# Attention maxima in float16, one product per half batch, and turns of queries, keys and sums in other slots

## What is computed

```python
k_mem, v_mem = jnp.split(memory, 2, axis=2)
Q = _split_heads(query, NUM_HEADS) * dh ** (-0.5)
Kh = _split_heads(k_mem, NUM_HEADS)
Vh = _split_heads(v_mem, NUM_HEADS)
logits = jnp.einsum('bhqd,bhkd->bhqk', Q, Kh) + b
...
weights = jax.nn.softmax(logits, axis=-1)
out = jnp.einsum('bhqk,bhkd->bhqd', weights, Vh)
```

## Time and profile before

| what | value |
|---|---|
| median of 3 runs | 3341.56 us (3337.22 to 3347.16) |
| the profiled execution | 3335.4 us, its span 3333.7 us |
| mean granted clock of TensorE | 0.895 of full speed |
| busy share of the span | PE 77%, DVE 68%, ACT 37%, POOL 28% |
| maxima in l0a | 64.9 to 289.4 us |
| maxima in l2a | 1711.3 to 1888.1 us |
| maxima in l2s | 2046.6 to 2253.4 us |
| maxima in l3a | 2980.9 to 3158.4 us |

### The profile page before, as it was taken

The page is one execution under the profiler, slowest core; times in us unless marked ns, Lnnn a source line. Parts: engine busy times, 40 slices in busy tenths (PEclk is TensorE's granted clock), DMA queues, the critical chain, the costliest instruction groups (busy, mean ns, idle before and its releaser), DMA issues. The chain is left out here.

```text
span 3333.7 us, 58668 instructions
## 1 busy us (share of the span) xinstructions
PE 2558.5 (77%) x21348; PEld 1660.5 (50%) x21348; DVE 2258.7 (68%) x5909; ACT 1245.9 (37%) x2228; POOL 924.7 (28%) x1324
## 2 busy tenths in 40 slices
PE   2997367999424367997989776996799999869962
PEld 1443355666323135886456543443565555546651
DVE  5997745666467434666677777997666555777768
ACT  1886334333122103111346564772322222226611
POOL 3442460100350520112655325871000000024200
PEclk9998689999757678999989987998799999889986
DMA  4330454222322215665631012100100000011001
GB/s 111 114 130 30 161 203 154 76 76 77 114 80 80 76 39 181 221 226 192 215 101 52 17 48 93 47 22 5 61 9 12 1 1 1 6 38 46 21 8 56
DMA packets 158163, 266.84 MB, mean 80 GB/s; under 512 B 22635, under 2 KB 106137, under 8 KB 151876
## 3 DMA queue, kind: packets, MB, share of 16 engines
q1 hardware_dynamic: 131204, 186.97, 16.9%
q0 software_dynamic: 17904, 76.23, 6.8%
q10 hardware_dynamic: 8784, 0.04, 0.2%
HBM read 175.25 MB, written 88.34 MB: 79 GB/s over the span
## 5 line engine op out<-in xcount | busy, mean ns | idle before, releaser
L1380 ACT ACTIVATE l2e_hf<-l2e_H 128x512 f32<-128x512 f32 x208 | 124.2, 597 | 375.9 <-PE l2e_H L1336 375.9
L1416 DVE CAST l2e_hh<-l2e_hf 128x512 f16<-128x512 f32 x208 | 88.7, 427 | 127.1 <-ACT l2e_hf L1380 112.0
L688 DVE TENSOR_REDUCE l0a_mx<-l0a_S 128x2 f32<-128x512 f32 x256 | 164.3, 682 | 11.9 <-PE l0a_S L530 11.2
L1336 PE MATMUL l2e_H<-l2o_hi,l2e_w 128*128 128x512 f16 x576 | 151.8, 382 | 14.9 <-DVE l2e_w L1392 14.9
L637 ACT ACTIVATE l0a_pf<-l0a_ST 128x512 f32<-128x512 f32 x256 | 145.9, 598 | 40.5 <-PE l0a_ST L544 34.8
L228 POOL TENSOR_TENSOR l3in_n_rstd<-l3in_n_sq,all_mhalf 128x8 f32<-128x8 f32 x4 | 6.9, 1724 | 553.8 <-DVE l3in_n_sq L152 553.8
L1336 PE MATMUL l2e_H<-l2e_hh,l2e_w 128*128 128x512 f16 x640 | 155.1, 379 | 0.0
L684 DVE CUSTOM_DVE_ANT_0 l2s_masked<-l2s_S,l2s_mq 128x128 f32<-128x128 f32 (+1 forms) x512 | 150.7, 349 | 6.1 <-PE l2s_S L530 5.7
L1380 ACT ACTIVATE l0e_hf<-l0e_H 128x512 f32<-128x512 f32 x128 | 76.4, 597 | 206.7 <-PE l0e_H L1336 206.7
L1336 PE MATMUL l1e_H<-l1b_hi,l1e_w 128*128 128x256 f16 (+1 forms) x936 | 145.4, 275 | 7.8 <-DMA l1e_w<-packed,all_second_weight_row 7.8
L1418 DVE TENSOR_TENSOR l2e_hl<-l2e_hf,l2e_hh 128x512 f16<-128x512 f32 x208 | 144.0, 692 | 7.2
(11 more groups left out here) (726 smaller groups left out, 7448.6 us busy)
## 6 DMA issues: line engine op xcount, KB each, us to landing
l0e_wf<-in_L_ffn_w SPq DMA_DIRECT2D x16, 1024.0 KB, 7.2
rows<-l0a_zeros SPq DMA_DIRECT2D x16, 640.0 KB, 6.1
l1u_rb<-rows SPq DMA_DIRECT2D x20, 512.0 KB, 4.7
results<-l1e_y SPq DMA_DIRECT2D x39, 256.0 KB, 3.9
l0a_kv<-in_ctx SPq DMA_DIRECT2D x16, 512.0 KB, 4.3
rows<-l0a_zeros SPq DMA_DIRECT2D x16, 512.0 KB
l0d_p_cx<-in_ctx SPq DMA_DIRECT2D x16, 512.0 KB, 5.8
l0u_rb<-rows SPq DMA_DIRECT2D x16, 512.0 KB, 5.7
```

The lines of the kernel that those rows point to most:

```text
L688: m = nc.vector.tensor_reduce(mx[h % 2][:, :, i], ps[:, :].rearrange("p (u k) -> p u k", u=TB), AX.X, ALU.max)
L1336: mm = pe.matmul(bank[0:fn, :], W[par][0:kn, at + k * wd + f0:at + k * wd + f0 + fn], X, start=(done == 0), stop=(done == k_all - 1))
L1380: nc.scalar.activation(hf[q % 4][0:fn, :], pair_of(q, lay)[0][0:fn, :], lay.func, scale=1.0 / WS).then_inc(acted, 1)
L1416: nc.vector.tensor_copy(high, v).then_inc(hi_done, 1)
```

## The change

It alters `attention_stage` in four ways. The maxima `mx` are written as float16 by the instructions that find them; `bound` and `nm` are gone, and `turn_max` turns `mx` itself, in float16, into the float16 bank. The two products of `divide` are one with 256 columns (`on` has its dimensions in another order for that, and POOL's `add` reads it so). `turn` is split into `turn_queries` and `turn_keys`, which have slots of their own. And the slots are others: with 16 heads the maxima are turned in slot 2 (before 1), the queries in 5 and the keys in 7 (before both in 4), the copy of the maxima is in slot 4 (before 3), the division in 3 (before 4). With 8 heads the sums are turned in slot 1 (before 2), the maxima in 1 (before 0), queries and keys in 3 (before 2), the copy of the maxima is in slot 2 (before 1). SP's transfers of the maxima follow that copy's slot.

```diff
-    BACK_AT, MAX_AT, TURN_AT = (1, 1, 4) if heads == 16 else (2, 0, 2)
-    COPY_AT, DIV_AT, KEYS_AT, SUM_AT = (3, 4, 1, 5) if heads == 16 else (1, 3, 1, 3)
+    BACK_AT, MAX_AT, TURN_Q_AT, TURN_K_AT = (1, 2, 5, 7) if heads == 16 else (1, 1, 3, 3)
+    COPY_AT, DIV_AT, KEYS_AT, SUM_AT = (4, 3, 1, 5) if heads == 16 else (2, 3, 1, 3)
...
-        mx = [st.sb(f"mx{i}", [P, TB, HALF]) for i in range(2)]
-        nm = [st.sb(f"nm{i}", [P, TB, HALF]) for i in range(2)]
+        mx = [st.sb(f"mx{i}", [P, TB, HALF], F16) for i in range(2)]
...
+                def turn_keys(h):
+                    if h:
                         pe.wait_ge(k_turned, h)
...
                 def turn_max(h):
-                    pe.wait_ge(nm_set, h + 1)
+                    pe.wait_ge(maxed, (h + 1) * HALF)
                     pe.wait_ge(q_turned, min(h + 3, NH))
                     for u in range(TB):
-                        m = pe.transpose(N_ps[0:HALF, u, :], nm[h % 2][:, u, :], g.ident[:, :])
+                        m = pe.transpose(N_ps[0:HALF, u, :], mx[h % 2][:, u, :], ident_h[:, :])
...
-                def bound(h):
-                    dve.wait_ge(maxed, (h + 1) * HALF)
-                    if h >= 2:
-                        dve.wait_ge(nm_turned, h - 1)
-                    nc.vector.tensor_scalar(nm[h % 2][:, :, :], mx[h % 2][:, :, :], -NEG_H, NEG_H, ALU.min, ALU.max
-                                            ).then_inc(nm_set, 1)
...
+                    nc.vector.tensor_tensor(
+                        dst, sums[..., 0:dh], by.unsqueeze(len(by.shape)).to_broadcast(list(by.shape) + [dh]),
+                        ALU.mult).then_inc(o_mul, 1)
```

More of the change, by code:

```diff
@@ L362, in attention_stage @@
         rs = st.sb("rs", [P, 2 * TB, G])
-        on = [st.sb(f"on{i}", [P, TB, P]) for i in range(2)]
+        on = [st.sb(f"on{i}", [P, 2, TB, P // 2]) for i in range(2)]
         ident_h = st.sb("ident_h", [P, P], F16)
@@ L369, in attention_stage @@
         MH_ps = [st.ps(f"M{i}", [P, 8, P], F16) for i in range(2)]
-        N_ps = MH_ps[0][:, :, :].rearrange("p a b -> p (a b)").bitcast(F32).rearrange("p (a b) -> p a b", b=P)
+        N_ps = MH_ps[0]
         if causal:
@@ L380, in attention_stage @@
         scored, maxed = st.sem("scored"), st.sem("maxed")
-        nm_set, nm_turned, nm_rows = st.sem("nm_set"), st.sem("nm_turned"), st.sem("nm_rows")
+        nm_turned, nm_rows = st.sem("nm_turned"), st.sem("nm_rows")
         nm_in = [st.sem(f"nm_in{i}") for i in range(2)]
@@ L497, in add @@
                     b = h // 2
-                    x = g.x[:, b * TB:(b + 1) * TB, h % 2 * P:h % 2 * P + P]
+                    x = g.x[:, b * TB:(b + 1) * TB, h % 2 * P:h % 2 * P + P].rearrange("p u (s c) -> p s u c", s=2)
                     pool.wait_ge(o_mul, h + 1)
-                    nc.gpsimd.tensor_tensor(out=x, in0=x, in1=on[h % 2][:, :, :], op=ALU.add).then_inc(o_done, 1)
+                    nc.gpsimd.tensor_tensor(out=x, in0=x, in1=on[h % 2][:, :, :, :], op=ALU.add).then_inc(o_done, 1)
                 for j, i, n in slots():
@@ L565, in weigh, with turn, turn_queries @@
                         m.then_inc(weighed, 1)
-                def turn(h):
+                def turn(h, i):
+                    v = (qs, ks)[i][h // 2 % 2][:, :, :, :].rearrange("p t h r -> p t (h r)")
+                    for c in range(4):
+                        for u in range(TB):
+                            j = h % 2 * 4 + c
+                            m = pe.transpose(MH_ps[i][:, c * TB + u, :], v[:, u, j * P:j * P + P], ident_h[:, :])
+                    m.then_inc(chunks, 1)
+                def turn_queries(h):
                     b = h // 2
@@ L577, in turn @@
                         pe.wait_ge(q_turned, h)
+                    turn(h, 0)
+                def turn_keys(h):
+                    if h:
                         pe.wait_ge(k_turned, h)
[L579 to L585, removed]
+                    turn(h, 1)
                 def turn_max(h):
-                    pe.wait_ge(nm_set, h + 1)
+                    pe.wait_ge(maxed, (h + 1) * HALF)
                     pe.wait_ge(q_turned, min(h + 3, NH))
                     for u in range(TB):
-                        m = pe.transpose(N_ps[0:HALF, u, :], nm[h % 2][:, u, :], g.ident[:, :])
+                        m = pe.transpose(N_ps[0:HALF, u, :], mx[h % 2][:, u, :], ident_h[:, :])
                     m.then_inc(nm_turned, 1)
@@ L615, in _ @@
                         turn_max(j - 1)
-                    if i == TURN_AT and 0 <= j + 2 < NH:
-                        turn(j + 2)
+                    if i == TURN_Q_AT and 0 <= j + 2 < NH:
+                        turn_queries(j + 2)
+                    if i == TURN_K_AT and 0 <= j + 2 < NH:
+                        turn_keys(j + 2)
             @block.scalar
@@ L675, in maxima @@
                     if i == 0 and h >= 2:
-                        dve.wait_ge(nm_set, h - 1)
+                        dve.wait_ge(nm_turned, h - 1)
                     ps = S_ps[n % 2]
@@ L715, in divide @@
                         dve.wait_ge(o_done, h - 1)
[L716 to L724, removed]
+                    if out_res is None:
+                        dst = on[h % 2][:, :, :, :].rearrange("p s u (g d) -> p (s u) g d", d=dh)
+                    else:
+                        dst = out_res[:, b * TB:(b + 1) * TB, h % 2 * P:h % 2 * P + P].rearrange(
+                            "p u (s g d) -> p s u g d", s=2, d=dh)
+                        sums = sums.rearrange("p (s u) g e -> p s u g e", s=2)
+                    by = rs[:, :, :] if out_res is None else rs[:, :, :].rearrange("p (s u) g -> p s u g", s=2)
+                    nc.vector.tensor_tensor(
+                        dst, sums[..., 0:dh], by.unsqueeze(len(by.shape)).to_broadcast(list(by.shape) + [dh]),
+                        ALU.mult).then_inc(o_mul, 1)
                 for j, i, n in slots():
-                    if i == 0 and 0 <= j - 1 < NH:
-                        bound(j - 1)
                     if i == 0 and 0 <= j + 1 < NH:
```

## The result

The changed kernel takes 3334.7 us (median of 12 runs, 3329.91 to 3338.47) against 3342.77 (12 runs, 3337.22 to 3347.46): ratio 0.9976, 95% interval 0.9968 to 0.9985. It is 8 us faster, which is less than the 0.3% that the prediction called tellable, but with 12 runs each the interval excludes 1; it is within 1 us of the 3334 us forecast. The span of its profiled execution is 3328.8 us, 4.9 less than before.

The account below looks back on a forecast made before the run. It took the DVE–PE loop through two score buffers to bound the 16-head stages and PE's row the 8-head ones. 8.4 + 7.0 - 21.8 = -6.4 us, taken as -7.5 from 3341.56, gave 3334 us, range 3308 to 3350.

Parts of the forecast that it names:

- The main claim: 16-head stages: loop between DVE and PE gets longer despite lighter DVE work, l0a +8.4 us, l2s +7.0; chance 0.50.
- The 0.73 us of the prediction: l0a, DVE's row: 0.73 us saved per half batch, leaving 6.23 us of work; the saving turns into waits for scores.
- Rival B: 16-head stages: DVE's full row decides and the two score buffers absorb the rest; -24.0 us there, 3296 in all; chance 0.18.
- C: 16-head loop: merged product keeps 0.49 us and copy of the maxima 0.33; +15.7 us, 3350 in all; chance 0.14.
- D: 8 heads: turn of the maxima still waits, so 0.19 us stay; 10.6 us more, 3345 in all; chance 0.06.
- The loop: 16 heads: chain from slot 3's scores round to the next half batch; 7.35 us in l0a, 6.73 in l2s.
- Weighing 0.58: l0a, PE part of the loop: the weighing ahead of the turn of the maxima takes 0.58 us.
- the DVE part: l0a loop, slot 3's scores through division, copy and slot 4's maximum until PE starts: 2.66 us.
- Start and end: Half batches where weighing or division is missing: lighter DVE row gains about 0.6 us in each of four, -2.5 us.
- the pair falls from 0.22 to 0.11 us: PE: two turns of the maxima, float16 instead of float32, save 0.11 us per half batch with 8 heads.
- the 0.19 us of waiting: 8 heads, PE: the wait for the query copy ahead of the turn of the maxima goes, 0.19 us per half batch.
- the separate turns of the 64-row stages: 16 heads, PE: turning queries and keys separately costs one more gap pair, about 0.2 us per half batch.

Follow-up runs that it names:

- e3: Changed kernel, with 16 heads the copy of the maxima back in slot 3 and the division in slot 4: 3313.78 us, ratio 0.9933 to the kernel before.
- e5: Changed kernel with the product by the reciprocals in two instructions again: 3336.24 us, ratio 0.9986 to the kernel before.
- e2: Kernel before with the turns split and the changed kernel's slots, keeping clamp, float32 maxima and two products: 3363.32 us, ratio 1.0087.
- e1: Changed kernel's work (float16 maxima, no clamp, one product) in the slots of the kernel before: 3316.37 us, ratio 0.9942 to the kernel before.
- e7: Changed kernel with a 128-column tile of the maxima with 16 heads only: 3339.66 us, ratio 0.9993 to the kernel before.
- e9: Changed kernel with only the copy of the maxima back in slot 3 (16 heads): period 6.96 us in l0a, 6.43 in l2s.
- e10: Changed kernel with only the division back in slot 4 (16 heads): period 6.91 us in l0a, 6.43 in l2s.
- e4: Changed kernel with the tile of the maxima 128 columns wide, 8 heads only: 3323.51 us, ratio 0.9958 to the kernel before.

## Why the prediction was right, point by point

**The main claim held.** In the changed 16-head stages the lighter DVE row brings no gain, because the chain from the scores of slot 3 over division, copy and maximum to those of slot 6 and back over PE is longer than DVE's work. The period of l0a rose from 6.96 to 7.15 although DVE's row lost 0.28 us of work (clamp 0.08, product 0.07, copy 0.13; its busy time fell by 0.26). The 0.73 us of the prediction are 6.96 - 6.23, which counts gaps and waits of the row before as if they were work. e3 shows the place, and e5 that DVE time counts there in full. e2 shows that the longer product and copy lengthen the wait ahead of the turn of the queries by their 0.20 us. Rival B (DVE's row decides, 3296) falls: DVE's busy time went down to 90% of l0a. The reason given against B, that PE's rows are full in slots 7 to 2, is not what the trace before shows: PE idles 0.29 us ahead of the scores of slot 0, and this wait lies on the chain that set the period (e1). B has some truth in l2s, where e1 fell from 6.42 to 6.18 by the work alone, a part of the way to B's 5.92. Nor was C right: product and copy cost 0.34 and 0.20. Of D's mechanism nothing is seen; no wait for the query copy stands ahead of the turn of the maxima, and yet the 8-head period is as if it did (5.63 against 5.45 + 0.19), for another reason.

**The loop was over-long by 0.2 us.** 7.35 was forecast, 7.15 measured; in l2s 6.73 and 6.57. Two terms were mis-sized. "Weighing 0.58" ahead of the turn of the maxima is 0.45: 0.13 us (e7 gives it back, +0.12). And the DVE part is 2.59, not 2.66: PE starts 0.06 us behind the end of maximum 4, not 0.14. That the branch over the copy to the turn of the queries is as long was right; PE starts 0.10 us behind the copy there, and its idle time of 0.52 us was forecast as about 0.6. With 2.59 and 4.56 in place of 2.66 and 4.69 the sum is the measured 7.15.

**Start and end were under-sized for l0a.** -2.5 us were put there. The first four half batches took 31.6 us before and 26.1 after, -5.5 alone. In e1, with the old slots, they take 29.8. So most of it, 3.7 us, belongs to the slots and not to the lighter row, as the prediction had it. In e9, e10 and e3, which have the copy, the division or both back in the slots of before, they take 27.8, 27.9 and 28.0: about half of the 3.7 hangs on those two standing where they do in the changed kernel. With the shorter loop this makes -0.2 for l0a instead of +8.4; in l2s the same four half batches were 28.4 and 27.4, and one of them was longer than before (8.06 against 7.27): there the forecast -2.5 was not reached. With 8 heads it was about right: -2.2 and -2.4.

**The 8-head stages gave 12.2 us, not 21.8.** This is the step that failed, and it is the term "the pair falls from 0.22 to 0.11 us". The pair itself does (0.06 from turn to turn). But the prediction did not ask in which tiling a turn with 4 columns runs: behind the sums it starts 0.20 us after the last matmul instead of 0.11, and the scores follow 0.15 behind it instead of 0.06 (e4; behind the float32 turn 0.11). From the sums to the scores that is 0.41 us, 0.08 dearer than the 0.33 in float32, not 0.11 cheaper. The period came out 0.18 above the forecast 5.45, and e4 measures 5.43 without the two gaps. The other term, the 0.19 us of waiting, did go, but e1 shows that it goes in the old slots too. The Trainium skill, TensorEngine Tiling (Array Packing), Key Properties, says that a change of the tiling mode drains TensorE. The prediction weighed this rule for the separate turns of the 64-row stages and stopped there; the traces show the same gap in the 8-head stages (0.20 against 0.11 ahead of the turn), where the kernel before had none.

**Two errors cancelled.** The 16-head stages were forecast at +15.4 us and changed by +2.6, 12.8 better; the 8-head stages were forecast at -21.8 and changed by -12.2, 9.6 worse. Together the touched stages were 3.2 us better than forecast (-9.6 against -6.4), so the closeness of the total is luck. The mechanism, the loop, is confirmed by e3, e5, e9 and e10; the prices are confirmed on DVE, and on PE they were incomplete.

**What stays open.** Why l0a in e1 stays at 6.96 us is read from rows of two traces; no run took that loop apart. That the three effects make e2's 0.54 us is arithmetic from rows too, not an experiment of each, and why every second clamp lasts three times as long is not shown. Which chain shortened in l2s in e1 was not worked out. The 4.7 us in the untouched stages are a difference between two single executions; nothing ties them to the change.

## What to carry to other kernels

When two engines hand work over through two buffers, price an instruction by where it stands in the loop between them: follow one buffer all the way round, and add both engines' steps and the hand-over times. Work that stands between two hand-overs costs in full even if its engine is idle elsewhere, and moving it by one slot (e3: 0.43 us per half batch in l0a for two numbers) can be worth more than making it lighter (e1: nothing there). Look for every buffer that the moved work releases: here the sums, too, held PE. And the tiling of a small matmul or turn has to suit its neighbours: the narrow form is cheap behind narrow weights and dear behind full ones.

## What the runs showed of the hardware

- A float16 turn of 4 or 8 columns behaves as one of 32-column weights. Behind a weighing with 32-column weights it starts 0.20 us after the last matmul (a full-width one 0.31, e7), behind a weighing with 64-column weights 0.31 (e1), behind full-width float32 turns 0.20 (a full-width one 0.11, e4). Full-width scores follow it after 0.15 (behind a full-width turn after 0.06, e4), 64-row scores after 0.15 as behind any float16 turn.
- The float32 turn of the same 4 columns has no such gap: in e2 it starts 0.11 us behind the turn of the sums, and there and in the kernel before the full-width scores start 0.11 us behind it. The runs don't say what makes the difference between the two types.
- A product with 256 columns from PSUM by a broadcast factor lasts 0.42 us and lets the next instruction start after 0.34; two of 128 columns take 0.41 to the next start. The one instruction with the longer pattern costs 0.07 us less.
- A copy of 256 float16 elements out of PSUM takes 0.27 us, one of 256 float32 elements, written as float16, 0.40.
- From the end of a DVE instruction to the PE instruction that waits for it were 0.06 us (scores of slot 6 behind maximum 4, changed kernel and e9), 0.15 (scores of slot 0 behind maximum 6, the kernel before and e1), 0.10 (turn of the queries behind the copy) and 0.15 (weighing behind the product, e3 and e10).
